# Gather's first loads made into the Hadamard stage's weight buffer, and that stage's products in another order

## What is computed

```python
# L2_ffn: 4-bit-like quantised gate and up, Hadamard transform, quantised down
def quantize_act(x):
    scale = maximum(max(abs(x), axis=-1) / 7, 1e-8)
    return clip(round(x / scale), -8, 7) * scale
gate, up = split(quantize_act(x) @ wq.T)            # 4096 each
h = matmul_hadU(silu(gate) * up, 1 / sqrt(4096))    # Hadamard over 4096
out = quantize_act(h) @ wdq.T

# L3_xattn: for each of 1024 points its 16 nearest (by ctx), features gathered and weighed
idx = top_k(-pdist, 16)
lap = take_along_axis(feat, idx).reshape(Bn, 16, Nn * Fd)
out = einsum('bkm,k->bm', lap, affine_w) + affine_b[0]

# L3_ffn: 8 experts of rank 64, the two likeliest weighed
y = x @ lora_A[e].T @ lora_B[e].T
```

## Time and profile before

| what | us |
|---|---|
| median of 3 runs | 3226.4 (3213.05 to 3229.02) |
| the profiled execution, its time | 3231.9 |
| its span, first to last instruction | 3230.3 |
| busy: PE, DVE, ACT, POOL | 2800.1, 2008.1, 1186.7, 452.8 |
| mean granted TensorE clock | 0.929 of 2.4 GHz |

### The profile page before, as it was taken

One profiled execution on the slowest core, in us unless ns is written; L12 is line 12 of the kernel. 1 busy time (PEld: TensorE's weight loads), 2 busy tenths in 40 slices (PEclk: granted clock), 3 DMA queues, 4 the chain that ended last, 5 costly groups with the idle time before them and its releaser, 6 DMA issues. The chain is left out here.

```text
span 3230.3 us, 54176 instructions
## 1 busy us (share of the span) xinstructions
PE 2800.1 (87%) x20468; PEld 1972.8 (61%) x20468; DVE 2008.1 (62%) x3515; ACT 1186.7 (37%) x2604; POOL 452.8 (14%) x516
## 2 busy tenths in 40 slices
PE   7999999999994699978689999999578898847888
PEld 4665665665662588856355655655377777635664
DVE  5545545545535776654567777775457887846774
ACT  2333333333332233312245555554255545311222
POOL 0110110110112100000012222222122322200000
PEclk9999999999997799986789999999699998967999
DMA  6100100100105545544433333331230001045441
GB/s 240 45 33 12 44 33 12 44 33 11 39 1 197 156 128 146 134 100 171 142 125 135 117 121 135 129 111 64 70 136 24 19 19 30 13 115 182 163 146 47
DMA packets 103179, 292.18 MB, mean 90 GB/s; under 512 B 33480, under 2 KB 56680, under 8 KB 93456
## 3 DMA queue, kind: packets, MB, share of 16 engines
q1 hardware_dynamic: 75408, 220.09, 20.3%
q0 software_dynamic: 18704, 53.14, 5.6%
q10 hardware_dynamic: 8848, 16.10, 1.9%
HBM read 246.24 MB, written 43.04 MB: 90 GB/s over the span
## 5 line engine op out<-in xcount | busy, mean ns | idle before, releaser
L1462 DVE TENSOR_REDUCE latent_nmax<-bank 112x1 f32<-112x487 f32 x128 | 85.2, 665 | 274.4 <-PE bank L1327 266.9
L1846 POOL TENSOR_SCALAR grouped_probs<-grouped_probs,grouped_rsum 112x375 f32<-112x375 f32 x256 | 152.7, 616 | 721.7 <-DVE grouped_rsum L1900 721.7
L2092 PE MATMUL bank<-ffn_qT,ffn_wgu 128*128 128x112 bf16 x4096 | 219.9, 219 | 22.6 <-ACTq L2163 13.3
L2092 PEld LDWEIGHTS bank<-ffn_qT,ffn_wgu 128*128 128x128 fp8e4 x4096 | 217.0, 102 | 27.4 <-issue 25.0
L1288 PEld LDWEIGHTS bank<-latent_hT,latent_wq 128*128 128x128 f32 x1536 | 182.1, 197 | 10.7 <-issue 10.2
L2231 POOL TENSOR_TENSOR ffn_h<-ffn_sl,ffn_us 128x448 f32<-128x448 f32 x64 | 135.4, 2116 | 360.1 <-ACTq L2186 360.1
L1251 POOL TENSOR_SCALAR latent_probs<-latent_probs,latent_rsum 112x487 f32<-112x487 f32 x128 | 88.0, 687 | 665.2 <-DVE latent_rsum L1467 665.2
L1288 PE MATMUL bank<-latent_hT,latent_wq 128*128 128x112 f32 x1536 | 181.0, 279 | 0.0
L1896 DVE TENSOR_REDUCE grouped_nmax<-bank 112x1 f32<-112x375 f32 x256 | 122.4, 541 | 92.5 <-PE bank L1723 89.8
L1810 ACT ACTIVATE grouped_probs<-bank,grouped_nmax 112x375 f32<-112x375 f32 x256 | 143.3, 572 | 75.7 <-DVE grouped_nmax L1896 75.7
L1266 PE MATMUL bank<-latent_wv,latent_hT 128*125 128x384 f32 (+1 forms) x512 | 167.8, 489 | 0.0
(11 more groups left out here) (398 smaller groups left out, 5808.0 us busy)
## 6 DMA issues: line engine op xcount, KB each, us to landing
grouped_raw<-L_weights SPq DMA_DIRECT2D x24, 2048.0 KB, 8.1
points_spread<-numbers SPq DMA_DIRECT2D x32, 912.0 KB
codes<-grouped_code SPq DMA_DIRECT2D x24, 512.0 KB, 6.0
latent_hT<-ctxT SPq DMA_DIRECT2D x8, 1500.0 KB, 6.9
plain_ctxT<-ctxT POOLq DMA_DIRECT2D x8, 1500.0 KB, 17.9
plain_ctx<-ctx POOLq DMA_DIRECT2D x8, 1500.0 KB, 35.1
grouped_ctx<-ctxT SPq DMA_DIRECT2D x8, 1500.0 KB, 12.2
latent_xy<-planes SPq DMA_DIRECT2D x8, 1024.0 KB, 8.5
```

The source lines that it names most:

```text
L1846: pool.tensor_scalar(pr[:, g % 2, j, :], pr[:, g % 2, j, :], rsum[:, g % 2, j:j + 1], 1.0, ALU.mult, ALU.mult)\
L2092: mm = pe.matmul(ahead.tile(t)[:, i * Q:(i + 1) * Q], wgu[:, u0 + f // 4, c:c + P], qT[:, k, :], start=(k == 0), stop=(k == KC - 1))
```

## The change

It has four parts.

1. A class `GatherBuffers` owns one SBUF tensor, `gather_whole`, of the size of `wgu`. The Hadamard stage uses it as `wgu`. The Gather stage uses views of it: `spread`, `aT` and `bT`.
2. At the end of the Hadamard stage's program GpSimd waits for the last up tile's products and then issues the first batch's eight loads of `spread` and those of `aT` and `bT`. `gT` (32 KB), x of sample 0 and the constants are in an `Early` object, which SP loads in sequence 6. The five constants become one array of 128 x 73. `Scope` clears the semaphores of both at the Gather stage's end.
3. The Gather stage issues none of these loads. It clears only `z`'s four spare columns, not all of it. x of the other samples and `spread` of the other batches are loaded as before.
4. In a Hadamard sequence the order is another. TensorE: two tiles of `turned(b - 1)`, then `entered(b + 1)`, then the other two; the first half of `down` between steps 3 and 4 (it was between 2 and 3), the second behind step 7 (it was between 5 and 6). ScalarE's copies follow it. VectorE: half 0 of `finished` stands between steps 5 and 6 (it was ahead of the reduction, with step 4), half 1 behind `quantised` (it was ahead of it).

```diff
+class GatherBuffers:
+    def __init__(self, nc, ctx, numbers, A):
+        self.whole = ctx.enter_context(nc.sbuf_tensor("gather_whole", [P, 16, 4096], FP8))
+        flat = self.whole[:].rearrange("p u n -> p (u n)")
+        self.spread = flat[:, 0:32768].bitcast(BF16).rearrange("p (c n) -> p c n", c=4)
+        self.aT = flat[:, 32768:49152].bitcast(F32).rearrange("p (k n) -> p k n", k=KC)
+        self.bT = flat[:, 49152:65536].bitcast(F32).rearrange("p (k n) -> p k n", k=4)
...
+    def load_spread(self, eng, b, c, loaded):
+        for w, r0, n in ((0, 0, 114), (1, 114, 9)):
+            eng.dma_start(self.spread[r0:r0 + n, c, :], self.numbers[b, w, 32 * c:32 * (c + 1), :].rearrange("r c -> (r c)")
+                          .rearrange("(a n) -> a n", a=1).broadcast_to([n, 4 * D])).then_inc(loaded, 16)
+    def load_weights(self, eng):
+        eng.dma_start(self.aT, fold(self.A["L3_lora_AT"])).then_inc(self.weights_loaded, 16)
+        eng.dma_start(self.bT, fold(self.A["L3_lora_BT"])).then_inc(self.weights_loaded, 16)
...
 # hadamard_ffn, SP
                     if gate_up:
                         sp.dma_start(x[:, 1 - slot, :], x_in[b + 1]).then_inc(x_loaded[1 - slot], 16)
+                if gate_up and not quantise:
+                    early.load(sp)
 # TensorE
                 if not first:
-                    turned(b - 1)
+                    turned(b - 1, (0, 1))
                 if gate_up:
                     entered(b + 1, 1 - slot)
-                    gate_and_up(b + 1, lambda j: down(b - 1, j // 3 - 1) if j in (3, 6) and not first else None)
+                if not first:
+                    turned(b - 1, (2, 3))
+                if gate_up:
+                    gate_and_up(b + 1, lambda j: down(b - 1, 0) if j == 4 and not first else None)
+                    if not first:
+                        down(b - 1, 1)
 # GpSimd
             rounds(pool, sequence)
+            t = ("u", STEPS - 1)
+            pool.wait_ge(ahead.full(t), ahead.count(t, B - 1))
+            for c in range(4):
+                gather.load_spread(pool, 0, c, gather.first_loaded[c])
+            gather.load_weights(pool)
 # VectorE
                     butterfly(b, k)
-                    if k == 4 and not first:
-                        finished(b - 1, 1 - slot, turn + (slot - 1), 0)
                     if gate_up:
                         step(b + 1, k)
...
                     step(b + 1, 5)
+                if not first:
+                    finished(b - 1, 1 - slot, turn + (slot - 1), 0)
+                if gate_up:
                     step(b + 1, 6)
...
                 integers(hq[:], hb[:], rsh[:]).then_inc(hq_ready, 1)
+                if quantise:
+                    quantised(b + 2, slot)
                 if not first:
                     finished(b - 1, 1 - slot, turn + (slot - 1), 1)
-                if quantise:
-                    quantised(b + 2, slot)
 # gather_experts
-            sp.dma_start(x[:, 0, :], x_in[0]).then_inc(x_loaded[0], 16)
-            for b in range(B):
+            for b in range(1, B):
...
-            pool.wait_ge(onehot_ready, 6)
-            pool.dma_start(aT[:], fold(A["L3_lora_AT"])).then_inc(weights_loaded, 16)
-            pool.dma_start(gT[:], fold(A["L3_ffn_gate_wT"])).then_inc(weights_loaded, 16)
-            pool.dma_start(bT[:], fold(A["L3_lora_BT"])).then_inc(weights_loaded, 16)
...
-            act.dma_start(wcol[:], A["L3_xattn_affine_w"]).then_inc(consts_loaded, 16)
-            act.dma_start(sel[:], A["row_mask"]).then_inc(consts_loaded, 16)
-            act.dma_start(bias[:], rows(A["L3_xattn_affine_b"], P)).then_inc(consts_loaded, 16)
-            act.dma_start(count[:], A["count"]).then_inc(consts_loaded, 16)
-            act.dma_start(penalty[:], A["penalty"]).then_inc(consts_loaded, 16)
...
-            dve.memset(z[:], 0.0)
+            dve.memset(z[:, :, D:NA * CH], 0.0)
```

More of the change, by code:

```diff
@@ L2147, in _ @@
             rounds(pe, sequence)
[L2148 removed]
+            turned(B - 1, range(4))
             for i in range(2):
@@ L2196, in _, with turned @@
             act.drain().then_inc(sdb_ready, 1)
-            def turned(b):
-                for i in range(4):
+            def turned(b, tiles):
+                for i in tiles:
                     t = ("hT", i)
```

103 lines of the change are left out of this document (59 added, 44 removed).

## The result

The changed kernel takes 3173.8 us (median of 4 executions, 3170.2 to 3182.2) against 3227.7 for the one before in the same series: a ratio of 0.9839 with a 95% interval of 0.9811 to 0.9868. The forecast was 3171. The profiled execution took 3175.3 us, its span is 3173.6.

A forecast was written before the change was run, and what follows sets the result against it. No engine fills the span; VectorE nearly bounds the full Hadamard rounds (floor 53.2 us of 60.0), with TensorE near it. Terms of 24 + 0.5 + 16.9 + 14.3 = 55.7 us off the median 3226.4 gave 3171 us, range 3152 to 3198.

The forecast's parts named there:

- Term 1: Hadamard stage, five full rounds: each goes from 60.0 to 55.2 us, 24 us won, bounds 7 and 34.
- The walk: One full Hadamard round followed event by event from its first butterfly; the next butterfly starts at 55.2 us.
- I take the slow one, since TensorE still pauses ahead of it: First gate tile of a round: 3.0 us at the low clock, not 1.6 at full, so step 0 starts at 6.4.
- Term 2: Hadamard stage, short round of sequence 6, which quantises nothing: 55.2 against 55.82 us, 0.5 us won, bounds 0 and 3.
- Sequence 7 stays: End of the Hadamard stage: sequence 7 and what follows it stay at 61.6 us, nothing won.
- Term 3: Seam between the stages: data loaded early, first look 10.7 instead of 27.6 us in, 16.9 us won, bounds 14 and 18.
- Term 4: Gather stage, batch 1: 19.3 us of `spread` waits go, 5 us charged for late `back`; 14.3 won, bounds 8 and 19.3.
- B: Rival: pause and low clock move to the down product, Hadamard order gives only 7 us; 3188 us, chance 0.17.
- C: Rival: full rounds reach VectorE's floor, 34 us won there; 3159 us, with all bounds 3152; chance 0.12.
- D: Rival: loads still under way behind the seam, batch 1 waits as before; 3185 us, chance 0.05.
- E: Rival: GpSimd's loads are starved and land one after another, TensorE waits for aT and bT; about 3500 us, chance 0.04.
- The rule against the change: Loads on GpSimd's queue beside the last butterflies: VectorE's two-port modes keep GpSimd out, so loads wait for descriptors.

The follow-up runs named there:

- turn_back: The changed kernel with all four tiles of turned codes ahead of the activations again, on TensorE and ScalarE; ratio 0.9906 to the kernel before.
- five_ahead: The changed kernel with VectorE's step 5 ahead of the reduction instead of behind it; ratio 0.9813 to the kernel before.
- loads_only: The changed kernel with the Hadamard stage's old order, so only the loads and the seam are changed; ratio 0.9917 to the kernel before.

## Why the prediction was right

The time, 3171, is 3 us from the median, and the sum, 55.7, 1 us from the spans' difference. The terms are less good than that: the rounds were put too low and batch 1 too high, and the two errors cancel. That the total came so near is luck: the time's interval is 9 us to either side, and the start up to sequence 0, which varies by 30 us with the same code, differs by only 2.6 between the two profiles.

- **Term 1** (24, came as 28.2). The walk held event by event, except for its second step. From the first butterfly it has the first gate product at 3.4 (3.1 in the rows after), step 0 at 6.4 (4.9), 28.8 from step 0 to step 5 (28.75), the Hadamard products' start at 47.3 (45.6), the next butterfly at 55.2 (53.9). The step that failed is "I take the slow one, since TensorE still pauses ahead of it": the pause shrank from 1.94 to 0.63 us, and no low clock came behind it. That is 1.5 us a round, 7 in five. Its ground was too general as well: "after each of these pauses comes a stretch at 0.50 or 0.55" holds for the round that was read, but in the round from 2443.45 the same pause, 1.86 us, had none behind it (62 products in 3.21 us). turn_back shows the step from the other side: with 1.86 us of pause the 3.4 us at 0.56 of the clock return. The other way went the new pause ahead of gate tile 7: two of the five full rounds have a low stretch behind it and take 55.97 and 54.24 us, so the mean is 54.4. The two small copies moved, which the walk booked at 1.7 us, thus carry the largest part of the term (19.0 us when undone), and the moved down product, for which it gave the room, alone carries 1.3 us of all six rounds. These shares come from one trace each, and the old order differs by 9 us between two.
- **Term 2** (0.5, came as 1.4): within its bounds, but the same round takes 55.82 and 53.16 us in two executions of the old order, so neither number means much.
- **Sequence 7 stays** (0, came as +1.3). The two halves of the last down product take 16.48 us instead of 15.40, with the same 64 products: a longer stretch at the low clock, some 5 us instead of 3 (windows of 3 to 4 us). It was not in the sum.
- **Term 3** (16.9, came as 17.4) held as written, and is for the most part what is loaded early besides `spread`.
- **Term 4** (14.3, came as 9.9). `spread` was no longer waited for, as forecast. What failed is "I charge 5 us" for `back`: the wait was 7.13 on TensorE and 8.1 on VectorE. By the rows TensorE is ready to turn `back` 10.2 us after the store, not 12.1; the load was issued 6.9 us in and took 10.4. 2 to 3 us of the miss are that. The rest is not traced, and the spread between executions is as large.
- **From batch 2 on nothing changes** held within 1.4 us.
- **The rivals.** B (pause and low clock move to the down product) came in part and ahead of its place: in three of the six rounds the low clock lies over gate and up tile 7. The down products themselves take 7.07 us, as at the full clock in the earlier trace rows, and 28.2 us were won instead of 7. C (VectorE's floor) is what the rounds came close to, 28.2 of its 34 us; the total stayed above it through Term 4. D and E did not come.
- **The rule against the change.** GpSimd's products still took 2.8 to 3.0 us beside butterflies, and the loads on its queue landed in 13.8 (median of the four large ones of `spread`) to 33.7 us, bT faster than the 46.2 of the earlier trace rows. But all ten were issued in 5.9 us, from 2757.97 on, and VectorE had little to do there: it waited 6.56 us for the Hadamard tiles and began the butterflies at 2767.18. So the Trainium skill's rule (SBUF — State Buffer, SBUF: two separate sides) was not put to the test; whether loads issued in the midst of butterflies would be held up was not tried. The prediction also applied it too widely: the same page's section Who interferes with whom says that `tensor_tensor`, which the butterflies are, has no two-port mode, and that with both inputs in SBUF it holds up GpSimd's reads.

## What to carry over

A pause of TensorE costs more than its length where a stretch at the low clock follows: letting the copies that are wanted first go first started the gate products 1.9 us sooner and gave 3.3 us a round. Read several rounds and more than one execution before a low stretch is booked behind a pause: the same pause had one in five rounds of six, in two, or in all. When an order of three engines is changed, test each engine's part alone before believing a reason: here the most visible change, the 4.5 us pause inside the Hadamard products, was worth 1.3 us of six rounds. And when a wait goes and the time stays, look at the next engine's timeline just ahead of the same event: here a root with two table loads, moved to where ScalarE idled together with VectorE's steps for it, took 9 us off five_ahead's rounds.

## What the runs showed of the hardware

- The same code takes a different time from execution to execution in steps that go with the granted clock: the short round of the old order 55.82 us at 0.94 and 53.16 at 1.00.
- Behind a pause of 0.53 to 0.64 us ahead of the first gate product (and 0.34 at most shortly ahead of it) TensorE kept 1.00 in all six rounds after. Behind 1.69 to 2.03 us (and 0.91 to 0.99 shortly ahead) the clock fell in 13 of 18 rounds (before 5, loads_only 2, turn_back 6 of 6); in turn_back at 2613 it was 0.56 for 3.4 us. Behind 2.17 to 2.63 us ahead of gate tile 7 it fell in three of six rounds, and not in those with the longest pauses.
- While the 8 MB of the ten early loads moved, with some 1.5 MB of other traffic, the DMAs were busy for 0.92 of 40 us at 243 GB/s, above the 190 of the earlier trace rows. The window of all engines (length, busy of PE, PEld, DVE, ACT, POOL, clock, DMA share, GB/s):

```profile
2757.00:2797.00 40.00, 25.39 (x170) 18.15 (x168) 30.12 (x23) 8.13 (x12) 6.87 (x11) 0.90 0.92 243
```
